# First two blocks' rows kept on chip, statistics and the first gated product moved ahead at each block boundary, first two hidden products interleaved

## The reference

```python
x = x + mixer(layernorm(x))                        # 64 states for each channel, then W_out
x = x + xattn(ctx, ctx, layernorm(x))              # softmax over 64 keys, then W_out
h = silu(z @ w1.T * s1) * (z @ w2.T * s2)          # z = layernorm(x), 256 -> 1024
h = gelu(h @ h1.T * sh1); h = gelu(h @ h2.T * sh2) # 1024 -> 1024, exact gelu
x = x + h @ w3.T * s3                              # 1024 -> 256
```

## Time and profile before

| what | value |
|---|---|
| median of 3 runs | 955.03 us (954.43 to 955.85) |
| the profiled execution, its own time | 954.79 us |
| its span, first to last instruction | 953.0 us |
| PE busy | 877.2 us, 92% |
| DVE, ACT, POOL busy | 519.0, 495.5, 182.4 us |
| mean granted TensorE clock | 0.98 of full speed |
| length of a loop body from block 1 on | 99.4 us |

### The profile page before, as it was taken

One profiled execution on the slowest core, in us unless ns is written; L12 is line 12 of the kernel. 1 busy time (PEld: TensorE's weight loads), 2 busy tenths in 40 slices (PEclk: granted clock), 3 DMA queues, 4 the chain that ended last, 5 costly groups with the idle time before them and its releaser, 6 DMA issues.

```text
span 953.0 us, 15162 instructions
## 1 busy us (share of the span) xinstructions
PE 877.2 (92%) x5570; PEld 697.1 (73%) x5570; DVE 519.0 (54%) x927; ACT 495.5 (52%) x761; POOL 182.4 (19%) x201
## 2 busy tenths in 40 slices
PE   1079898999999999999999999999999999999996
PEld 0078876777777777777777777778778877777885
DVE  7996485555456454555555555554556465544411
ACT  2836542476356735663475536653675356636331
POOL 1567600500040003200230014000500050003000
PEclk9679999899999999999999999999999999999999
DMA  9971798500110001000200020001000110001000
GB/s 340 224 170 49 269 413 303 214 1 1 51 44 0 0 23 71 0 0 22 72 0 0 0 94 0 0 0 72 22 0 0 50 44 0 0 22 44 1 1 24
DMA packets 15784, 62.82 MB, mean 66 GB/s; under 512 B 2867, under 2 KB 4534, under 8 KB 14934
## 3 DMA queue, kind: packets, MB, share of 16 engines
q1 hardware_dynamic: 15718, 62.35, 19.2%
q0 software_dynamic: 32, 0.00, 0.0%
HBM read 50.16 MB, written 23.72 MB: 78 GB/s over the span
## 4 chain that ended last, share of the span: by engine, by line
PE 77%; DVE 11%; ACT 5%; issue 4%; DMA 1%; DVEq 0%; ACTq 0%; SPq 0%
PE pair L1182 47%; PE pair L1169 10%; PE pair L1118 3%; PE pair L1107 3%; PE pair L1134 3%; PE pair L539 2%; PE pair L470 2%; PE pair L1127 2%; PE pair L477 1%; PE pair L1074 1%; DVE red L932 1%; PE pair L484 1%; DVE vbuf L997 1%; DVE st L868 1%; DVE GG L337 1%
## 5 line engine op out<-in xcount | busy, mean ns | idle before, releaser
L803 ACT ACTIVATE vbuf<-pair,scl 128x512 f32<-128x512 f32 x128 | 87.8, 686 | 237.1 <-PE pair L1182 231.3
L1182 PE MATMUL pair<-h1hi,h_turned 128*128 128x512 f32 x512 | 204.0, 398 | 1.6 <-DVE h1lo L968 1.6
L1182 PE MATMUL pair<-h2hi,h_turned 128*128 128x512 f32 x512 | 202.6, 396 | 0.0
L1182 PE MATMUL pair<-h1lo,h_turned 128*128 128x512 f32 x512 | 199.8, 390 | 0.0
L1182 PE MATMUL pair<-h2lo,h_turned 128*128 128x512 f32 x512 | 199.6, 390 | 0.0
L968 DVE TENSOR_TENSOR h1lo<-vbuf,h1hi 128x512 fp32r<-128x512 f32 x80 | 57.7, 721 | 118.5 <-ACT h1hi L804 117.7
L1182 PEld LDWEIGHTS pair<-h1hi,h_turned 128*128 128x128 f32 x512 | 96.1, 188 | 34.3 <-issue 10.5
L1182 PEld LDWEIGHTS pair<-h2hi,h_turned 128*128 128x128 f32 x512 | 96.1, 188 | 25.2 <-issue 5.9
L968 DVE TENSOR_TENSOR h2lo<-vbuf,h2hi 128x512 fp32r<-128x512 f32 x64 | 44.2, 690 | 123.5 <-ACT h2hi L804 123.5
L1182 PEld LDWEIGHTS pair<-h2lo,h_turned 128*128 128x128 f32 x512 | 96.2, 188 | 19.3
L1182 PEld LDWEIGHTS pair<-h1lo,h_turned 128*128 128x128 f32 x512 | 96.2, 188 | 18.9
(11 more groups left out here) (138 smaller groups left out, 1455.0 us busy)
## 6 DMA issues: line engine op xcount, KB each, us to landing
h_turned<-d_h SPq DMA_DIRECT2D x2, 4096.0 KB, 16.0
xres<-in_x SPq DMA_DIRECT2D x8, 512.0 KB, 7.3
tok<-in_xs SPq DMA_DIRECT2D x8, 512.0 KB, 12.2
EE<-alpha_rows SPq DMA_DIRECT2D x16, 256.0 KB, 11.6
ring<-kernel_rows SPq DMA_DIRECT2D x16, 256.0 KB, 4.4
x_rows<-x1t SPq DMA_DIRECT2D x8, 512.0 KB, 2.6
xr<-x_rows SPq DMA_DIRECT2D x8, 512.0 KB, 3.5
out<-xr SPq DMA_DIRECT2D x16, 256.0 KB, 2.1
```

The costliest lines, as they stand in the source:

```text
L803: e.activation(vb[:, s % 2, :], h_ps[s % 4], ACT.Gelu, scale=sc)
L1182: ins = e.matmul(bank, w[:, k, m * P:(m + 1) * P], src[part][:, k, :], start=(k == 0 and part == 0), stop=(k == HC - 1 and part == 1))
```

## The change

Four edits, in one diff:

1. Where x1 lies. Block 0's x1 stays in `xres` (the mixer's residual buffer), and DVE's `x1_add` for block 1 writes straight into `x1t`. Block 1's store to DRAM and its load back are gone. The load of the h2 weights, which go over `xres`, now also waits for block 0's last readers.
2. DVE's order at a boundary. `stats` of the next attention and the first gated product `gate(j, 0)` move from the start of the next body to the end of this one, ahead of the residual sum (`xr`). For this the last loop body is written out.
3. PE's order at a boundary. `gated_first` of the next block is issued before `turn_out`; it waits for the two output evacuations (`o_ev`) one by one. The output columns go through `prob` in place of `sg`.
4. The hidden part's start. `hidden_first` makes products 0 and 1 together: the input pieces 0 to 6 of both, then piece 7 of both. On DVE `normalised(j, 0)` (the first softmax division) comes ahead of the first h2 difference.

```diff
--- before.py
+++ after.py
@@ -443,7 +443,7 @@
         e.wait_ge(base_b, 4 * i + 4)
         e.wait_ge(pr_ps, i + 1)
         v = xres[:, 4 * i:4 * i + 4, :].rearrange("p j d -> p (j d)")
-        e.tensor_tensor(v, p_bank(i)[:, :], v, ALU.add).then_inc(x1a, 1)
+        e.tensor_tensor(t["x1t"][:, :] if i == 1 else v, p_bank(i)[:, :], v, ALU.add).then_inc(x1a, 1)
...
@@ -612,6 +612,9 @@
     VALUES_AT = [6, 12]
     block = ctx.enter_context(nc.Block())
 
+    def rows(j):
+        return m["xres"][:, 0:TPB, :].rearrange("p j d -> p (j d)") if isinstance(j, int) and j == 0 else x1t[:, :]
...
@@ -620,7 +623,7 @@
         m["sync_mixer"](e)
 
         def attn_loads(j):
-            if not (isinstance(j, int) and j == 0):
+            if not (isinstance(j, int) and j < 2):
                 e.wait_ge(S["x2_st"], 16 * j)
                 e.sem_inc(S["step_s2"], 1)
                 e.wait_ge(S["nat_rdy"], 8 * j)
@@ -632,7 +635,7 @@
 
         def x2_store(j):
             e.wait_ge(S["x2_rdy"], j + 1)
-            e.dma_start(blk_rows(x2d, j), x1t[:, :]).then_inc(S["x2_st"], 16)
+            e.dma_start(blk_rows(x2d, j), rows(j)).then_inc(S["x2_st"], 16)
...
@@ -647,16 +650,16 @@
         attn_loads(0)
         e.dma_start(xbo[:, :], a["xb"].partition_broadcast(P)).then_inc(S["xbo_in"], 16)
         m["sync_core"](e)
-        m["x1_store"](e, 1)
         m["sync_hidden"](e)
         for i in range(2, 6):
             m["x1_store"](e, i)
+        attn_loads(1)
         x2_store(0)
-        e.wait_ge(m["x1_st"], 80)
-        attn_loads(1)
         for i in range(6, NBLK):
             m["x1_store"](e, i)
-        e.wait_ge(m["x1_st"], 16 * (NBLK - 1))
+        e.wait_ge(m["x1_st"], 16 * (NBLK - 2))
+        e.wait_ge(S["x2_st"], 16)
+        e.wait_ge(S["nat_rdy"], 8)
         e.wait_ge(m["h2_d"], 16)
         e.dma_start(t["h2"].bitcast(F32), t["dh2"]).then_inc(S["h2_in"], 16)
...
@@ -805,7 +808,7 @@
 
         def out_evac(i, m):
             e.wait_ge(S["mm"], 26 * i + (25 + m))
-            e.activation(sg[:, m, :], h_ps[m], ACT.Copy, scale=sc3[:, m:m + 1]).then_inc(S["o_ev"], 1)
+            e.activation(prob[:, m, :], h_ps[m], ACT.Copy, scale=sc3[:, m:m + 1]).then_inc(S["o_ev"], 1)
...
@@ -875,13 +878,14 @@
             e.tensor_scalar_add(ve, mv[:, :, 1], EPS).then_inc(S["var_rdy"], 1)
 
         def normed(n):
+            src = rows(0 if isinstance(n, int) and n < 2 else 1)
...
@@ -898,7 +902,8 @@
                     e.wait_ge(m["p0_ps"], 1)
                 elif k == 2:
                     e.wait_ge(m["pr_ps"], 1)
-                e.tensor_tensor(x1t[:, k * DM:(k + 1) * DM], pair[3][:, k * DM:(k + 1) * DM], m["xres"][:, k, :], ALU.add).then_inc(S["x1_tile"], 1)
+                v = m["xres"][:, k, :]
+                e.tensor_tensor(v, pair[3][:, k * DM:(k + 1) * DM], v, ALU.add).then_inc(S["x1_tile"], 1)
...
@@ -986,16 +991,16 @@
             e.wait_ge(S["folded"], 1)
             e.tensor_reduce(most[:, :], bits[:, :], AX.X, ALU.max).then_inc(S["folded"], 1)
 
-        def body(i, attn):
+        def gate(i, m):
+            e.wait_ge(S["sg_rdy"], 8 * i + (m + 1))
+            e.wait_ge(S["lo"], 24 * i + max(m - 1, 0))
+            e.scalar_tensor_tensor(vb[:, m % 2, :], pair[m % 2][:, 512:1024], sc2[:, m:m + 1], sg[:, m % 2, :],
+                                   ALU.mult, ALU.mult).then_inc(S["v_rdy"], 1)
+
+        def body(i, attn, more):
             j = i + 1
-            if attn:
-                e.wait_ge(S["x1_in"], 16 * j)
-                stats(2 * j)
-            for m in range(HC):
-                e.wait_ge(S["sg_rdy"], 8 * i + (m + 1))
-                e.wait_ge(S["lo"], 24 * i + max(m - 1, 0))
-                e.scalar_tensor_tensor(vb[:, m % 2, :], pair[m % 2][:, 512:1024], sc2[:, m:m + 1], sg[:, m % 2, :],
-                                       ALU.mult, ALU.mult).then_inc(S["v_rdy"], 1)
+            for m in range(1, HC):
+                gate(i, m)
                 if m == HC - 1:
                     e.wait_ge(S["lo"], 24 * i + m - 1)
                     low(i, m - 1, h1)
@@ -1006,12 +1011,14 @@
                 maxima(j, 0)
                 shifted(j, 0)
             for s in range(2 * HC):
+                if attn and s == 0:
+                    normalised(j, 0)
                 low(i, HC + s, h2 if s < HC else h1)
                 if attn and s in TURN and s != TURN[3]:
                     shifted(j, TURN.index(s) + 1)
                 if attn and s + 1 in TURN and s + 1 != TURN[3]:
                     maxima(j, TURN.index(s + 1) + 1)
-                if attn and s + 2 in TURN:
+                if attn and s > 0 and s + 2 in TURN:
                     normalised(j, TURN.index(s + 2))
                 if attn and s == 13:
                     residual(j)
@@ -1028,6 +1035,11 @@
                     e.tensor_reduce(t["flag"][:, :], bit_row, AX.X, ALU.max).then_inc(S["flagged"], 1)
             if attn:
                 z_lo(j)
+            if more:
+                e.wait_ge(S["x1_in"], 16 * j)
+                stats(2 * j + 2)
+            if attn:
+                gate(j, 0)
             e.wait_ge(S["xr_in"], 16 * i + 16)
             for k in range(2):
                 here = slice(k * BLK, (k + 1) * BLK)
@@ -1057,10 +1069,14 @@
         x1_add(e, 6)
         normed(1)
         z_lo(0)
+        e.wait_ge(m["x1a"], 1)
+        stats(2)
         x1_add(e, 7)
-        with e.Fori(0, NBLK - 1) as i:
-            body(i, True)
-        body(NBLK - 1, False)
+        gate(0, 0)
+        with e.Fori(0, NBLK - 2) as i:
+            body(i, True, True)
+        body(NBLK - 2, True, False)
+        body(NBLK - 1, False, False)
 
...
@@ -1147,8 +1163,9 @@
 
         def gated_first(i):
             e.wait_ge(S["z_hi"], DH * i + DH)
-            e.wait_ge(S["o_ev"], 2 * i)
             for g, w in enumerate((w1T, w2T)):
+                if not isinstance(i, int):
+                    e.wait_ge(S["o_ev"], 2 * i - (1 - g))
                 for part in range(2):
                     if g == 0 and part == 1:
                         e.wait_ge(S["z_lo"], DH * i + DH)
@@ -1158,9 +1175,6 @@
             ins.then_inc(S["mm"], 1)
 
...
         def gated(i, m):
-            if m == 0:
-                gated_first(i)
-                return
             if m >= 2:
...
@@ -1183,10 +1197,21 @@
                                    start=(k == 0 and part == 0), stop=(k == HC - 1 and part == 1))
             ins.then_inc(S["mm"], 1)
 
+        def hidden_first(i):
+            e.wait_ge(S["v_rdy"], 8 * i + 7)
+            for ks in (range(HC - 1), (HC - 1,)):
+                for m in range(2):
+                    for k in ks:
+                        if m == 0:
+                            e.wait_ge(S["lo"], 24 * i + (k + 1))
+                        for part in range(2):
+                            ins = e.matmul(h_ps[m], h1T[:, k, m * P:(m + 1) * P], h1[part][:, k, :],
+                                           start=(k == 0 and part == 0), stop=(k == HC - 1 and part == 1))
+                    if k == HC - 1:
+                        ins.then_inc(S["mm"], 1)
+
         def hidden(i, s):
-            if s < 2:
-                e.wait_ge(S["v_rdy"], 8 * i + 7)
-            elif s < 4:
+            if s < 4:
                 e.wait_ge(S["v_rdy"], 8 * i + 8)
             else:
                 e.wait_ge(S["hi"], 24 * i + (HC + s - 3))
@@ -1200,20 +1225,22 @@
             for k in range(DH):
                 e.wait_ge(S["o_ev"], 2 * i + (k + 1))
                 for m in range(TPB):
-                    ins = e.transpose(pair[2][:, m * DM + k * P:m * DM + (k + 1) * P], sg[:, k, m * P:(m + 1) * P], ident[:, :])
+                    ins = e.transpose(pair[2][:, m * DM + k * P:m * DM + (k + 1) * P], prob[:, k, m * P:(m + 1) * P], ident[:, :])
                     if k == DH - 1 and m % 2 == 1:
                         ins.then_inc(S["o_t"], 1)
 
         def body(i, attn):
             j = i + 1
-            for m in range(HC):
+            for m in range(1, HC):
                 gated(i, m)
                 if attn and m == 3:
                     turn_q(j)
                 if attn and m == 6:
                     scores(j, 0)
-            for s in range(2 * HC):
-                hidden(i, s)
+            hidden_first(i)
+            for s in range(1, 2 * HC):
+                if s > 1:
+                    hidden(i, s)
                 if attn and s in TURN:
                     turn_p(j, TURN.index(s))
                 if attn and s in SCORES_AT:
@@ -1226,6 +1253,8 @@
             if attn:
                 turn_z(j)
             last(i, 1)
+            if attn:
+                gated_first(j)
             turn_out(i)
...
@@ -1266,6 +1295,7 @@
         lead_turn(1)
         y_project(e, 7, second)
         e.wait_ge(m["w_in"], 64)
+        gated_first(0)
         with e.Fori(0, NBLK - 1) as i:
             body(i, True)
         body(NBLK - 1, False)
```

(8 more changed lines are left out.)

## The result

The changed kernel takes 942.76 us (median of 4 runs, 942.59 to 943.58) where the kernel before took 954.88 (4 runs, 954.43 to 955.85): ratio 0.9882, 95% interval 0.9862 to 0.9901. It gained 12.1 us, where 16.5 were forecast and the range ended at 942.5. The profiled execution took 942.65 us with a span of 940.9; PE is busy 92% of it, as in the earlier trace rows.

The account below looks back on a forecast made before the run. PE, busy 92% of the span, was taken as the bound, with only its gaps to win. Loop start 6.5, boundaries 6 x 0.43 + 0.5 and hidden start twice 7 x 0.49 gave 16.5 us, so 938.5 us; range 935.0 to 942.5.

Parts of the forecast that it names:

- Start of the loop: At the loop's start PE's 4.41 us stop shrinks to about 0.7 and the clock stays up: 6.5 us gained.
- Boundary: From the first step behind a block's last product to the next query transposes: 0.43 us gained at each of six boundaries.
- The sum: All terms over the whole kernel: 6.5 + 6 x 0.43 + 0.5 + 7 x 0.49 + 7 x 0.49 = 16.5 us gained.
- The rule on the ports: At nat beside POOL: DVE and GpSimd share a port pair, locked per instruction by the first starter; nat kept at 2.30 us.
- Boundary into block 7: At the boundary without query transposes PE's own gaps go: 0.5 us gained.
- Hidden start: At each hidden part's start, interleaved h1 products gain 0.49 us and the earlier softmax division 0.49 us, seven times each.
- clock: Rival at the loop's start: the clock falls even at the shorter wait, costing 2.6 us: 941.1 us; chance 0.09.
- tables: Rival at the boundary: second Silu or DVE's second product no earlier, from late table or residual sum; 2.6 lost, 941.1; chance 0.07.
- hidden start: Rival at the hidden part's start: one wait is traded for another, 3.4 us lost: 941.9 us; chance 0.08.
- late load: Rival at the boundary: statistics wait for the x1 load, gated product behind them; slower than before, 962 at 14 us; chance 0.02.
- `nat` ahead of POOL: Rival at the boundary: nat starts before POOL's subtraction, so the 0.4 us wait goes; 2.8 us more gained, 935.7; chance 0.10.

Follow-up runs that it names:

- the first three experiments: Changed kernel with, one at a time: POOL's second subtraction held until nat is written, 936.92 us; nat at the boundary, 935.13; first subtraction on DVE, 935.96.

## Why the prediction was wrong

- **Start of the loop, 6.5 us: right, 6.7.** The stop became 0.38 us (about 0.7 was forecast), and the clock stayed up. The two kernels with the stop put back show both parts of it.
- **Boundary, 6 x 0.43 us: wrong, the failed step.** It was "Both follow the same Silu, POOL 1.29 and DVE 1.39 us behind it, so I keep 2.30 us". That looked only at the first subtraction. The second hangs on the next Silu, and that one comes earlier by the very wait the change removes. The prediction's own numbers had it: with no stop ahead of m = 2 the next Silu is due eight matmuls, 1.8 us, behind the second, and POOL's subtraction on it 1.29 + 1.8 = 3.1 us behind, ahead of the end of `nat` at 3.7. Measured: `nat` 3.17 us, a wait of 0.98 where 0.4 was written, the boundary 0.20 longer, not 0.43 shorter: 6 x 0.63 = 3.8 us. That two subtractions in place of one do it is shown by the first three experiments. The rest of the boundary was sound, and a little better than forecast: the second Silu came 4.89 us behind the zero (5.1 forecast), the load of x1 was in time, DVE idled 2.54 us. With one collision in `nat` the boundary is 8.64 us (8.96 forecast) and a body 97.64; with none they are 8.46 and 97.40.
- **Two figures of the prediction.** A body before is 99.34 us by the trace (274.45 to 373.79, from query transposes to query transposes), not 99.4, so its forecast should read 97.9, not 98.0. And with the wait gone its own starts give 9.39 - 8.55 = 0.84 us, where 0.9 is written; 0.93 was measured.
- **The sum.** The profiled spans differ by 953.0 - 940.9 = 12.1 us. The changed kernel's execution had 0.6 more of lead-in, so from the first gated product to the end it is 12.7: 6.7 to block 1's query transposes; 4.5 from there over six bodies (forecast 6 x 1.41 = 8.5); 1.5 behind them. That 4.0 is missing in the six bodies is the boundary's 3.8 and 0.2 more, which stays open.
- **The rule on the ports.** The trace first: `nat` alone 1.38 us, with one subtraction 2.10 to 2.34, with two 3.14 to 3.27, and the reverse, POOL at 1.36 to 1.49 when DVE was in first. The Trainium skill (SBUF — State Buffer, the part on the two sides and their ports) calls the shared pair an exclusive lock that the first to start holds for its whole instruction. The trace agrees, with the numbers above: of the four pieces of `nat`, each an instruction, only the one that starts inside a subtraction is long (1.24 and 1.36 us against 0.40). The prediction used the rule for one instruction, and saw in it only a possible gain.
- **Boundary into block 7, 0.5 us:** no stop is left there. It was not measured alone; with one hidden start (0.98) it was to give 1.5 us, and 1.5 is what the part behind the last query transposes gained.
- **Hidden start, 7 x 0.49 twice: right.** 0.49 us per body more with the interleave undone, 1.02 with the division undone, where the prediction had said that half of edit 4 alone would gain nothing; no wait is left in the changed kernel.
- **The rivals:** clock, tables, hidden start and late load did not come; the first Silu started 2.31 us behind the zero (358.85), as the row in the prediction had it (2.3), and not at 3.6. `nat` ahead of POOL did not either, in the changed kernel. What came was its mirror image, a second collision, which no rival named; hence the range ended 0.3 us too low. That the result lies so near the range is in part luck: the terms at the start and at the boundary that came out better than forecast made up for some of it.

## What to carry to other kernels

When a wait is removed, follow not only the instruction that waited but everything released by the same engine one and two steps later, and lay it beside the instructions with which it shares something. A duration read from the trace is valid only with the neighbours that it had there: count how many of another engine's instructions fall into it before and after. Where an elementwise pass sits on the path and collides, look for a stretch where its engine and the other are both idle; here moving it 5 us forward was worth 7.6 us, more than half of the 12.1 that the whole change gave.

## What the runs showed of the hardware

- DVE's four-piece fp32 tensor_scalar (128x256 each) beside POOL's tensor_tensor (1.29 us): 1.38, 2.22 and 3.17 us with none, one and two of them. Whoever starts later waits: a piece of 0.40 us takes 1.13 to 1.46, the subtraction 1.36 to 1.49. Some hundredths of a us in the start turned 1 us of a body, in two of six boundaries of one execution.
- Granted clock behind a stop of PE at the start of the loop: 1.00 after 0.38 and 1.93 us, 0.50 after 2.75, 4.41 and 5.14 us, for 5 to 6 us of work, at a price of 2.4 to 2.9 us beside the stop. Apart from 0.38 these are single executions, and the one of 1.93 us stood one product later.
- The first gated product came between 159.2 and 162.2 us in the profiled executions, while bodies 1 to 5 of one kernel repeat to 0.1 us where no collision flips. So bodies tell edits apart that medians of five runs don't.
